# Attention scores on TensorE: matmuls of 64 rows by 32 stationary columns in place of 64 by 128

## The reference

```
x = x + layer0(x)          # bias table given, mask over keys
x = x + layer1(x)          # q, k normalised; bias from a small network of the distance
q  = ln(x) @ Wq            # 512 -> 16 heads * 64
kv = ln(x) @ Wkv           # 512 -> 64 + 64, one null key and value put in front
sim = q @ k.T (+ bias, causal, mask); attn = softmax(sim)
out = ln((attn @ v) @ Wout)
```

## Time and profile before

| | |
|---|---|
| time, median of 3 runs | 2373.95 us (2372.37 to 2376.77) |
| span of the profiled execution, first to last instruction | 2374.7 us |
| PE busy | 2331.3 us, 98% |
| PEld busy | 2042.9 us, 86% |
| DVE / ACT / POOL busy | 68% / 67% / 38% |
| mean granted clock of PE | 0.992 |

### The profile page before, as it was taken

The page is one execution under the profiler, slowest core; times in us unless marked ns, Lnnn a source line. Parts: engine busy times, 40 slices in busy tenths (PEclk is TensorE's granted clock), DMA queues, the critical chain, the costliest instruction groups (busy, mean ns, idle before and its releaser), DMA issues.

```text
span 2374.7 us, 55130 instructions
## 1 busy us (share of the span) xinstructions
PE 2331.3 (98%) x17435; PEld 2042.9 (86%) x17435; DVE 1609.1 (68%) x4513; ACT 1596.8 (67%) x6497; POOL 912.5 (38%) x1702
## 2 busy tenths in 40 slices
PE   5899999999999999999999999999999999999998
PEld 5788888888888888888888888888888888888877
DVE  6666677667667667666666676676676676676666
ACT  4667666667666667666666666676666676666666
POOL 3234334334333433433443343343334334334332
PEclk8999999999999999999999999999999999999999
DMA  7111121111111111111111111111211111211111
GB/s 242 40 48 53 41 61 48 48 56 45 49 61 43 48 56 46 52 58 46 47 56 42 56 48 48 56 46 48 61 43 51 54 45 52 61 43 48 57 39 38
DMA packets 107251, 129.50 MB, mean 55 GB/s; under 512 B 45664, under 2 KB 49840, under 8 KB 107216
## 3 DMA queue, kind: packets, MB, share of 16 engines
q1 hardware_dynamic: 105472, 127.92, 17.5%
q0 software_dynamic: 688, 1.14, 0.2%
q10 hardware_dynamic: 1056, 0.00, 0.0%
HBM read 81.79 MB, written 33.57 MB: 49 GB/s over the span
## 4 chain that ended last, share of the span: by engine, by line
PE 95%; SPq 2%; ACT 1%; DVE 1%; POOL 1%; DMA 0%; issue 0%; POOLq 0%; DVEq 0%
PE psum L716 30%; PE psum L612 17%; PE psum L580 15%; PE psum L702 10%; PE psum L668 10%; PE psum L679 6%; PE psum L537 3%; PE psum L629 2%; PE psum L591 2%; SPq L389 1%; DMA keep<-in_mask_BxS_bk_dram 0%; ACT probs L872 0%; POOL masked_bias L1351 0%; SPq L478 0%; PE psum L620 0%
## 5 line engine op out<-in xcount | busy, mean ns | idle before, releaser
L1364 POOL TENSOR_TENSOR weights<-probs,den_inv 128x256 f32<-128x256 f32 (+3 forms) x1024 | 472.8, 489 | 1412.7 <-DVE den_inv L1094 1408.6
L872 ACT ACTIVATE probs<-probs,neg_max 128x129 f32<-128x129 f32 (+3 forms) x2048 | 716.2, 352 | 309.1 <-DVE neg_max L1088 309.1
L1081 DVE TENSOR_TENSOR probs<-psum,masked_bias 128x324 f32<-128x324 f32 x512 | 225.7, 483 | 271.3 <-PE psum L668 270.3
L1351 POOL TENSOR_TENSOR masked_bias<-bias,pad_neg 128x516 f32<-128x516 f32 (+3 forms) x512 | 396.9, 808 | 13.7 <-POOL pad_neg L1347 4.9
L872 ACT ACTIVATION_READ_ACCUMULATOR probs<-probs,neg_max 128x1 f32 x2048 | 385.7, 188 | 0.0
L716 PE MATMUL psum<-wo_hi,o_hi 128*128 128x512 f32 x1024 | 272.5, 408 | 0.8 <-issue 0.8
L716 PE MATMUL psum<-wo_hi,o_lo 128*128 128x512 f32 x1024 | 267.7, 403 | 0.8 <-DVE o_lo L1099 0.8
L1088 DVE TENSOR_REDUCE neg_max<-probs 128x2 f32<-128x258 f32 (+3 forms) x1024 | 256.9, 313 | 4.4
L716 PE MATMUL psum<-wo_lo,o_hi 128*128 128x512 f32 x1024 | 259.6, 395 | 0.0
L879 ACT COPY probs_t<-psum 128x384 f32<-128x384 f32 (+1 forms) x512 | 192.6, 429 | 78.0 <-PE psum L679 78.0
L716 PEld LDWEIGHTS psum<-wo_lo,o_hi 128*128 128x128 f32 x1024 | 192.4, 188 | 46.6
(11 more groups left out here) (138 smaller groups left out, 4397.0 us busy)
## 6 DMA issues: line engine op xcount, KB each, us to landing
res<-in_x_dram SPq DMA_DIRECT2D x64, 256.0 KB, 2.6
x_of<-y_out SPq DMA_DIRECT2D x64, 256.0 KB, 2.1
res<-x_of SPq DMA_DIRECT2D x64, 256.0 KB, 2.7
out_dram<-y_out SPq DMA_DIRECT2D x64, 256.0 KB, 2.1
xa<-in_x_dram SPq DMA_DIRECT2D x63, 256.0 KB, 2.6
xa<-x_of SPq DMA_DIRECT2D x63, 256.0 KB, 2.8
q_aside<-qp SPq DMA_DIRECT2D x32, 256.0 KB, 2.8
w_raw<-in_L_cond_Wq_dram SPq DMA_DIRECT2D x8, 512.0 KB, 8.6
```

Source lines behind the costliest of these rows:

```text
L872: x_ = nc.scalar.activation(s, s, ACT.Exp, bias=neg_max[:, g, k, e:e + 1], accum_out=den[:, g, k, e:e + 1])
L1081: a = nc.vector.tensor_tensor(probs[:, 2 * c + e, :], SB[c][e][:, 0:ROW], masked_bias[:, 2 * c + e, :], ALU.add)
L1351: m = nc.gpsimd.tensor_tensor(block(masked_bias, b), block(bias[u.layer], b), pad_neg[u.layer][:, 0:WIDTH[b]].unsqueeze(1).to_broadcast([P ...
L1364: m = nc.gpsimd.tensor_tensor(places[b], block(pairs(probs, g // 2), b)[:, :, 1:1 + n], den_inv[:, g, k, :].unsqueeze(2).to_broadcast([P, ...
```

## The change

Each score matmul of 64 rows by 128 stationary columns is cut into four of 64 rows by 32 columns (TR = 32). They write the same places of the same PSUM banks: strip r takes 32 stationary columns, and so 32 partitions of the output. Strips and halves alternate, so that eight neighbours in the program use eight different parts of the array. The moving operand is the same for the four strips of a half. In the loop, PE also adds one to a new semaphore, `pe_passed`, behind the waits of `scores`; nobody waits for it.

```diff
+TR = 32
...
+                if not isinstance(u.done, int):
+                    pe.sem_inc(pe_passed, 1)
                 for b in (3, 2, 1, 0):
-                    for e in range(2):
-                        half = slice(e * DH, (e + 1) * DH)
-                        k = keys[half, 0:WIDTH[b]] if u.layer else (kv_t, k_high)[e][half, u.odd, 0:WIDTH[b]]
-                        m = nc.tensor.matmul(block(SB[c][e], b), queries(u, c, half, b), k, start=True, stop=True)
+                    for r in range(0, P, TR):
+                        for e in range(2):
+                            half = slice(e * DH, (e + 1) * DH)
+                            k = keys[half, 0:WIDTH[b]] if u.layer else (kv_t, k_high)[e][half, u.odd, 0:WIDTH[b]]
+                            m = nc.tensor.matmul(block(SB[c][e], b)[r:r + TR, :], queries(u, c, half, b)[:, r:r + TR], k,
+                                                 start=True, stop=True)
                 m.then_inc(scores_done[c], 1)
```

More of the change, by code:

```diff
@@ L341, in build @@
             sem(n) for n in ("y_done", "bn_out_done", "mv_out_done", "ln_out_done", "rstd_out_done", "y_read", "out_done"))
-        sp_passed, dve_passed, pool_passed = sem("sp_passed"), sem("dve_passed"), sem("pool_passed")
+        sp_passed, dve_passed, pool_passed, pe_passed = sem("sp_passed"), sem("dve_passed"), sem("pool_passed"), sem("pe_passed")
         null_loaded, gain_loaded, null_row_loaded, null_v_loaded, g_out_loaded, rest_loaded, w1_loaded = (
```

## The result

The changed kernel takes 2554.1 us (2552.8 to 2555.3 in four runs), against 2374.6 us for the kernel before in the same comparison: a ratio of 1.0756, 95% interval 1.0740 to 1.0771. The forecast of 2420 us had the right sign and the wrong size; the time lies 44 us above its range. The profiled execution has a span of 2552.2 us, 177.5 us more than before.

The account below looks back on a forecast made before the run. PE was taken to bound the kernel, its scores set by weight loads. 2374.7 - 64 (saving) + 84 (instruction fetch waits) + 25 (clock) = 2420 us, own range 2375 to 2520, 8 in 10 for 2300 to 2510 us.

Parts of the forecast that it names:

- What bounds the kernel: Whole loop: PE waits for nobody, so its microseconds are the total's; weight loads set the scores' 1.91 us a unit.
- That the program does not fit: PE's loop: 1,940 instructions, 7.6 pieces, touching nine or ten, miss at each branch back; 0.65 given to not fitting.
- The price of a miss: At the branch and inside the first scores: waits of 1.2 and 1.8 us a pass, 28 passes, 84 us lost.
- The clock: Behind the idle stretches of each pass: granted clock falls one time in three, 25 us lost.
- The saving: Scores: parts of the array run side by side, saving 0.50 us a unit (0.30 to 0.61), 64 us.
- What is late next: Softmax between scores and transposes: POOL's weights are tightest, one unit in four waits, 0 to 3 us, taken as 0.
- The semaphore step at 0: PE's sequencer before the scores: new step covered by queued `values`, ends 0 and 40 us, taken as 0.
- a fitting loop: Rival: PE's loop is still held, only the saving is left, 2311 us (2297 to 2337); chance 0.28.
- One short wait: Rival: at the branch, `values` hides most, 1.3 us a pass, clock unaffected, 2347 us (2325 to 2372); chance 0.20.
- The strips that take turns: Rival: in the scores, strips cannot pass each other, 2.19 us for 1.70, 63 us lost, 2437 us or more; chance 0.07.

Follow-up runs that it names:

- 132 moving columns: Kernel before, 128 stationary columns, with the loop's score matmuls cut to 33 keys of each block, other keys left out: 2376.7 us (before 2376.8).
- 1,749 instructions: Changed kernel with 32-column strips in three of a pass's four units, the odd layer-0 unit keeping 128 columns: 2357.7 us, ratio 0.9926.
- 1,845: Changed kernel with only the second half of the odd layer-0 unit's scores kept at 128 columns: 2553.2 us, ratio 1.0751.
- straight code: Changed kernel with PE's loop passes written out, no branch back, strips kept, semaphore step gone: 2361.9 us, ratio 0.9939 to the kernel before.
- The narrow run: Changed kernel, 32-column strips, with the loop's score matmuls cut to 33 keys of each block, other keys left out: 2510.4 us (before 2376.8).

## Why the prediction came out wrong, step by step

**What bounds the kernel: right.** PE alone set the pace, 128 columns were bound by their loads (the stage was 1.91 us with 324 and with 132 moving columns), and a microsecond of PE was one of the total: 6.5 us a pass times 28 are the loss.

**That the program does not fit: right**, and the mechanism as forecast: packets on PE's instruction queue in each pass, a gap before the first scores and one inside them, the clock behind it. The Trainium skill (Runtime: NRT & Kernel Launch, Instruction fetch mechanics) gives PE 128 KiB in blocks of 16 KiB, which makes eight. The runs agree: 1,749 instructions stay, 1,845 do not, and about eight pieces were held. The same section also says that a taken branch waits for a fetch if its target isn't in a window of two pages; the prediction left that out, and it does not hold here, where a loop of 4.6 pieces already reads nothing again.

**The price of a miss: the first term that was mis-sized.** Forecast 1.2 + 1.8 = 3.0 us a pass, 84 us; measured 2.50 + 2.62 = 5.1 us, 143 us, near the upper end that I had set at 5.4. (Over all passes it is 5.0 us, 2.2 + 2.8 in the mean.) Three assumptions failed. I took the second piece as asked for partly along with the first; the 3.1 and 3.3 us from restart to the end of the second gap, with different work in between, and the place of the two packets say that it is asked for after. I took 2.7 us for a fetch; the branch's own record, not counted as busy, is 3.3 to 3.9 us long in the trace, 3.5 in the median (0.21 us before). And I had nothing for the way from the branch to the first matmul, which is 0.47 to 0.48 us in every pass. The cover was right: the branch's record starts 1.82 to 1.83 us before `values` ends, so `values` hid nearly all of its 1.88 us. For the pass shown that is 3.85 + 0.48 - 1.83 = 2.50 us, its first gap.

**The clock: the second.** Forecast a fall in one pass of three, 25 us; it fell in every pass, with some 1.96 us each: 55 us over 28. The mean granted clock of the run went from 0.992 to 0.957. The price of one fall was somewhat less than the 2.7 taken; the frequency was what failed. The example of before that I used followed idle of 2.83 us; here 5.1 us of idle come with only 0.45 us of work in between. I had a gap of about the same length, with a fall behind it, in the rows, and still gave it one third. The trace of before has a second one, near its end, which I did not use: idle of 2.27 us, less than the 3.0 us in two pieces that I forecast, and again the lower level behind it (timeline of PE; window: us, busy, clock, DMA share, GB/s):

```profile
2287.80 1.40 PE L679 MATMUL psum<-ident,weights 128*128 128x128 f32 x5 [2.27 <-POOL weights L1364]
```

```profile
2288.00:2290.00 2.00, 1.34 (x7) 0.50 0.00 0
```

Both of PE's idle stretches of over 2 us from the start of the loop on have a fall behind them; one in three had no row for it.

**The saving: the third.** Forecast 0.50 us a unit with ends 0.30 and 0.61, all of it between first and last matmul; measured 0.14 in the loop and 0.24 in straight code, 18 us in place of 64. Only 0.05 us of the 0.14 lie between first and last matmul (0.15 in straight code). Side by side was right, and so was 0.01 us between neighbours as a rounded figure. But my upper end took it that 0.16 us for 16 records sets the pace of the narrow blocks and nothing that of all. The narrow run gives 0.565 us for a half of 64 records, where the moving columns need 0.22. The reading that fits, inferred and not shown, is that the weight loads, as many as the matmuls, need instructions as well, and that PE executes faster than they come once the stock is used up. The other part is the pause between the halves, 0.15 us in the changed kernel and 0.04 in straight code; what makes it is open. The Trainium skill (TensorEngine Tiling (Array Packing), Performance Considerations, Instruction Overhead) warns against tiling further where a dimension is small already. Its advice fits the outcome, 64 columns at 1.37 us beating 32 at 1.77; its 60 cycles (25 ns) for each matmul, if paid one after the other, do not: 8.8 ns per record were measured. Whether each part of the array pays them for itself, side by side with the others, no run here shows.

**What is late next: right for this kernel, wrong for a faster one.** I had POOL's weights as the tightest place and 0 to 3 us. With 64 columns, where 0.54 us are in fact saved, it was DVE's `q_sb`, for about 10 us.

**The semaphore step at 0: right** in the kernel before (ratio 1.0000). In straight code the stage did not move either; 4.9 us of the total have no place there.

**The sum with measured terms:** 2374.7 - 18 + 143 + 55 = 2555 us, against a span of 2552.2. Of the 135 us between the forecast and this sum, 59 are the price of a miss, 30 the clock and 46 the saving. The three errors had one sign; the range had added up their ends only in part.

The rivals: a fitting loop is what the kernel with 1,749 instructions shows, with strips in three units of four: 2358 us. The 2311 forecast for strips in all four would be out of reach even so, since the saving was overrated. One short wait fell, as both waits are full. The strips that take turns fell by the timeline.

## What to carry to other kernels

Count the instructions of a loop body on the engine that sets the pace before making matmuls smaller: here 1,749 a pass cost nothing and 1,845 cost 195 us, since a loop that is a little too long is read anew in full, with two fetches of 3 to 4 us at its head and a fall of the clock behind them. Splitting the stationary columns pays only up to a point, as it seems until the instructions themselves become the pace: 64 columns took 0.54 us off a stage of 1.91, 32 columns only 0.14. Keep one tile width within a stage.

## What was not expected of the hardware

- With 96 instructions more than a loop that fits, the pass does not read one piece anew but all nine.
- Straight code with the same matmuls reads 193 packets of instructions in 1850 us and waits 9.2 us for them in all; the loop reads 237 and waits 119.8 us.
- Changing from 128 to 64 stationary columns and back, in both halves, costs a stage of 1.4 us about 0.4 us.
- In the half with few moving columns, PE starts 32 matmul records of 32 columns in 0.16 us, and the next 32, behind a pause of 0.08 us, in 0.32 us.
